# Layer 0 of a graph kernel: VectorE sums the logits before it weights the gathered values

## The reference

```python
h = relu(layernorm(x))
rowE, colE = h[rows], h[cols]
qE, kE, vE = rowE @ Wq, colE @ Wk, colE @ Wv          # (edges, 8, 16) each
att = clip(einsum('ehd,ehd->eh', qE, kE), -10, 10)
expAtt = exp(att)
att = expAtt / (segment_sum(expAtt, rows)[rows] + 1e-8)
res = segment_sum(att[..., None] * vE, rows) + h
x = x + layernorm(res) * gamma + beta
```

## Time and profile before

| | us |
|---|---|
| median of three executions | 5158.91 (5149.98 to 5164.05) |
| the profiled execution | 5157.34 |
| its span, first to last instruction | 5155.6 |
| first gather of layer 0 starts | 695.3 |
| last gather of layer 0 starts | 2854.3 |
| VectorE busy, TensorE busy, GpSimd busy over the span | 4088.8, 3914.0, 3437.0 |
| granted TensorE clock, mean over the span | 0.793 |

### The profile page before, as it was taken

How to read it: one execution, slowest core, us unless ns; L and a number is a source line. 1 busy time by engine, 2 the same in 40 slices (tenths; PEclk the granted TensorE clock), 3 DMA queues, 4 the chain that set the end, 5 groups by cost and what they waited for, 6 DMA issues and landing times. The chain is left out here.

```text
span 5155.6 us, 103185 instructions
## 1 busy us (share of the span) xinstructions
PE 3914.0 (76%) x22945; PEld 3311.6 (64%) x22946; DVE 4088.8 (79%) x12174; ACT 2438.7 (47%) x8516; POOL 3437.0 (67%) x3467
## 2 busy tenths in 40 slices
PE   5999967777877777788877167777778777778776
PEld 2788845565655666566655157777777777777775
DVE  7999968888888888888888667777776777777776
ACT  3999931111111111111111556766666676666674
POOL 0233357777777777777777167777777777777773
PEclk7999977767677666766677578888887898888897
DMA  1000023333333333333333032222222222222222
GB/s 48 15 26 23 19 81 114 114 116 113 114 114 113 116 113 114 113 115 114 113 114 114 19 86 68 66 68 66 66 68 64 66 68 66 66 68 63 66 69 54
DMA packets 202323, 411.53 MB, mean 80 GB/s; under 512 B 64713, under 2 KB 93612, under 8 KB 202096
## 3 DMA queue, kind: packets, MB, share of 16 engines
q0 software_dynamic: 136896, 330.76, 24.8%
q1 hardware_dynamic: 63364, 74.63, 4.6%
q10 hardware_dynamic: 1836, 4.03, 0.3%
HBM read 363.51 MB, written 42.45 MB: 79 GB/s over the span
## 5 line engine op out<-in xcount | busy, mean ns | idle before, releaser
L872 POOL DMA_INDIRECT h_rows<-h_table,idx_ring x1668 | 1586.8, 951 | 652.2 <-issue 473.1
L872 POOL DMA_INDIRECT kv_rows<-kv_table,idx_ring x1668 | 1652.1, 990 | 514.8 <-issue 507.8
L1068 PE MATMUL psum<-vx,hot 128*128 128x136 f32 x3336 | 860.0, 401 | 394.3 <-DVE acc L1098 380.9
L1068 PEld LDWEIGHTS psum<-vx,hot 128*128 128x128 f32 x3336 | 659.1, 272 | 577.0 <-DVE acc L1098 549.0
L1533 DVE SCALAR_TENSOR_TENSOR h_sb<-h_sb,corr,psum 128x129 f32 x1668 | 582.0, 349 | 515.3 <-PE psum L1490 231.7
L1021 ACT ACTIVATE vx<-clip 128x32 f32<-128x32 f32 x417 | 95.6, 229 | 1796.5 <-DVE clip L1140 1796.5
L1057 PE MATMUL psum<-q_sb,hotT 128*128 x3336 | 700.5, 375 | 81.4 <-DVE prod L1113 66.1
L1057 PEld LDWEIGHTS psum<-q_sb,hotT 128*128 128x128 f32 x3336 | 596.5, 269 | 221.6 <-issue 221.6
L1480 PE MATMUL psum<-ident,hotl 128*128 128x128 f32 x1668 | 316.1, 321 | 482.4 <-DVE highs L1559 480.9
L1098 DVE TENSOR_TENSOR acc<-acc,psum 128x136 f32 x1668 | 484.3, 290 | 159.5 <-issue 35.2
L1480 PEld LDWEIGHTS psum<-ident,hotl 128*128 128x128 f32 x1668 | 207.0, 160 | 549.5 <-issue 401.1
(11 more groups left out here) (221 smaller groups left out, 5788.6 us busy)
## 6 DMA issues: line engine op xcount, KB each, us to landing
kv_rows<-kv_table,idx_ring POOLq DMA_INDIRECT x1668
h_rows<-h_table,idx_ring POOLq DMA_INDIRECT x1668
own_rows<-own SPq DMA_DIRECT2D x104, 256.0 KB, 2.9
own<-own_rows SPq DMA_DIRECT2D x104, 256.0 KB
kv_table<-kv SPq DMA_DIRECT2D x21, 256.0 KB, 2.2
out<-q_sb SPq DMA_DIRECT2D x2, 1536.0 KB
h_sb<-h_now SPq DMA_DIRECT2D x21, 128.0 KB, 2.0
h_table<-acc SPq DMA_DIRECT2D x1, 1820.0 KB, 11.9
```

The source lines that it names most:

```text
L872: pool.indirect_dma_start(out=G[:, u, j, :], out_offset=None, in_=table, in_offset=bass.IndirectOffsetOnAxis(ap=idx[:, u, j:j + 1], axis=0 ...
L1068: last = nc.tensor.matmul(S_ps[j // HALF][:, j % HALF, :], hot[:, k, j * P:(j + 1) * P], vx[:, k, j, :], start=True, stop=True)
```

## The change

In VectorE's `step(i)` the sum of `prod` to `att` (L1128, with its waits for `s_prod` and `s_clip`) now stands directly behind `prod` of the same group, and `vx` of group i-2 (L1121) directly behind the sum. Nothing else is different: the same instructions, tiles, semaphores and counts.

```diff
                                             G[:, u, :, 0:D], ALU.mult).then_inc(s_prod, 1)
+                if inside(i):
+                    dve.wait_ge(s_prod, i + 1)
+                    need(dve, s_clip, i + 1 - NEAR)
+                    nc.vector.reduce_sum(att[:, u % NEAR, :],
+                                         prod[:, :].rearrange("p (a d) -> p a d", d=HD), AX_X).then_inc(s_red, 1)
                 if inside(i - 2):
                     k = (u - 2) % NEAR
                     dve.wait_ge(s_ex, i - 1)
...
                                             ALU.mult).then_inc(s_vx, 1)
-                if inside(i):
-                    dve.wait_ge(s_prod, i + 1)
-                    need(dve, s_clip, i + 1 - NEAR)
-                    nc.vector.reduce_sum(att[:, u % NEAR, :],
-                                         prod[:, :].rearrange("p (a d) -> p a d", d=HD), AX_X).then_inc(s_red, 1)
```

## The result

The changed kernel takes 5097.51 us (median of four, 5087.69 to 5107.58) against 5159.42 for the kernel before, a ratio of 0.9891 with a 95% interval of 0.9875 to 0.9906. So it is 62 us faster. The profiled execution took 5096.9 us, its span is 5095.2.

A forecast was written before the change was run, and what follows sets the result against it. Layer 0's gathers were taken as the bound: 417 groups x 0.16 us gives 67 us less, VectorE's added 50 us hidden, so 5157.3 - 67 = 5090 profiled, written as 5091 for the median; range 5078 to 5125 us.

The forecast's parts named there:

- The bound: Edges of layer 0: the stage takes as long as its 1668 gathers; VectorE's time costs nothing while it keeps up.
- The hold: A gather starting during `vx` or `hot` is held until 0.55 us behind that instruction's start; 73 us over the stage.
- the rule that it names beside them: Trainium skill: two-SBUF-input VectorE instruction and SBUF-reading GpSimd instruction contend; the second to start is blocked until the first is done.
- the sum does not: Rival: the sum also holds the gather that starts in it, +50 us, 5209 us; chance 0.03.
- The cost of the dependent pair: The sum waits for `prod` directly in front of it: 0.12 us a group, 50 us of VectorE's time, hidden.
- Room on VectorE: VectorE's idle time in front of `prod`: about 0.25 us a group left after the change, down from 0.47.
- The rival on the other side: Rival: `vx`, starting inside a running gather, waits for its end, 0.60 us late a group; +71 us, 5230; chance 0.06.
- The size: Layer 0 edges: a group takes 5.02 in place of 5.18 us, 67 us less of at most 73.
- the hold left in the groups with a register load: In two of eight groups `hot` may hold the gather at 3.47 by up to 0.12, some 0.02 us a group.
- The last gather: Sign in the changed kernel's timeline: the last gather of layer 0 at about 2787 us.
- that first group late by at most 0.1: First group of a turn, where registers come late: `prod` late by at most 0.1 us, catching up in the next group.

The follow-up runs named there:

- the pad: The order of before with one sum over 128 constant values (about 0.20 us) put between `prod` and `vx`: 5226.0 us, ratio 1.0143 to the kernel before.
- three gathers: Three gathers a group in place of four, the fourth tile's k and v constant: order of before 4940.98 us, changed order 4998.09 us.
- The kernel with the additions in front: The order of before with the first two additions of a group moved in front of `vx`: 5117.29 us, ratio 0.9930 to the kernel before.

## Why the prediction was right

**The bound.** Gathers bound the stage, VectorE does not. Shown by 0.20 us a group at its end, which cost nothing in either order, and by the stage's gain of 59.4 us, which is that of its gathers.

**The hold.** The gather that starts behind `vx` is held until 0.55 behind its start. Shown at three offsets, 0.37, 0.18 (with the pad) and 0.33 (`hot` in the changed kernel: 0.33 + 0.23 = 0.56), and taken away by taking `vx`'s second SBUF input away. `hot` does the same; the sum does not, with 404 gathers starting in it in the changed kernel. The hold ends before the instruction does: its row lasts 0.68 to 0.69, and its successor starts at 0.60. The prediction took the distance from the rows; a hold until the first is done, the rule that it names beside them, would be longer than the one measured.

**The cost of the dependent pair.** Forecast 0.12 and hidden; the sum is at 0.73, so it is 0.13, and it appeared as time only with three gathers, as 0.13 in the stage and 0.14 by the medians. With four gathers it is not free in the first group of a turn, as said below.

**Room on VectorE.** Forecast 0.25 us of idle time a group in front of `prod`; 68.4 us in 328 groups are 0.21.

**The rival on the other side.** A gather that has begun does not hold `vx`: in the plain groups it starts at 1.33 inside a running gather, and takes its 0.68. So this part of the rule that the prediction names does not come true here, and the measurement decides. It has a remnant, though, and only where the two start together. The kernel with the additions in front has such rows:

```profile
1219.84 0.72 DVE L1134 TENSOR_TENSOR hot<-slot_words,iota 128x512 f32<-128x512 f32 x1
1219.84 0.95 POOL L872 DMA_INDIRECT kv_rows<-kv_table,idx_ring  x1 [0.30 <-issue]
...
1220.49 0.30 DVE L1140 TENSOR_SCALAR clip<-att 128x32 f32<-128x32 f32 x1
```

Here the gather is plain, and it is `hot` that takes 0.72, with its successor 0.65 and not 0.60 behind its start. At 0.03 behind the gather, as in the earlier trace rows, it is 0.61 to 0.62, and from 0.05 on nothing is to be seen.

**The size.** Forecast 67 us of the possible 73, measured 62. The term that was too small is the hold left in the groups with a register load: I gave up to 0.12 in two of eight groups, 0.02 a group on average. It is 0.23 in one of eight, since `hot` there starts at 3.12 and not between 2.92 and 3.04. In the other of the two, u = 4, it starts at 2.89 (at 2.80 before, not at the 2.92 of the earlier trace rows) and holds nothing. Over the stage the gathers keep 1668 x 0.009 = 15 us of excess in place of 8, and these 7 us are what the stage lacks: 59.4 of 67. The last gather starts at 2796 us and not at 2787. The prediction also had that first group late by at most 0.1; from its `prod` to the next are 5.17 in place of 5.00. There the sum comes 0.81 behind `prod` rather than 0.72; why, no run here tells. It is the group at the begin of the Fori body. That its `prod` had not waited is not the reason: the next `prod`, at 1516.68, had not waited either, and its sum comes at 1517.40, 0.72 behind it.

## What to carry to other kernels

When two engines run locked to each other, look at what each instruction of the one starts inside of on the other, not only at who waits for whom: here no wait was recorded for the 73 us, only one gather in four that took 1.13 in place of 0.95. Compare median and mean of what should be equal, plot the duration against the distance to the other engine's last start, and then either move the instruction or take one of its two inputs from elsewhere. A new order that costs the engine time can win while that time is hidden, and loses (57 us here) as soon as it is not.

## What the runs showed of the hardware

- An indirect gather of 128 rows on GpSimd takes 946 ns and starts each 1.25 us; starting while a 512-column VectorE instruction with two SBUF inputs runs, it is held until 0.54 to 0.57 us behind that instruction's start, so by up to 0.37 in the rows shown. The other way round VectorE was held by 0.05 us at most, and only when it started within 0.04 us of the gather's start.
- A VectorE instruction of the same shape with one input from PSUM and one from SBUF, or a sum with one input from SBUF, holds nothing (404 gathers each). But two inputs are not the only way to hold one: between the layers of the kernel before, a gather that starts 0.47 behind the start of a memset of bf16 values, 1.45 long, takes 1.85 us in place of 0.94.
- A VectorE instruction that waits for the one directly in front of it starts 0.03 to 0.05 us behind its end, 0.12 to 0.13 later than an unrelated neighbour would (in the first group of each turn of the loop 0.13 behind its end, not explained).
